# Cross-attention over a 1500-key context: maxima with keys as partitions, queries and output projection inside the batch loop, loops written out

## The reference

```python
h = (x - mean(x)) * rsqrt(var(x) + 1e-5) * gamma + beta
Q = split_heads(h @ Wq.T)                     # 32 heads of 16
K = V = split_heads(ctx)
scores = where(mask, einsum('bhsd,bhtd->bhst', Q, K) / 4, -inf)
attn = einsum('bhst,bhtd->bhsd', softmax(scores), V)
out = x + merge_heads(attn) @ Wout.T
```

## Time and profile before

| | |
|---|---|
| three runs | 1756.49 us median (1751.47 to 1764.45) |
| profiled execution | 1757.97 us, its span 1756.3 us |
| TensorE matmul busy | 1492.5 us, 85% |
| VectorE busy | 1064.4 us, 61% |
| GpSimd busy | 866.0 us, 49% |
| ScalarE busy | 722.4 us, 41% |
| mean granted TensorE clock | 0.936 of 2.4 GHz |
| HBM traffic | 126 GB/s over the span |

### The profile page before, as it was taken

How to read it: one execution, slowest core, us unless ns; L and a number is a source line. 1 busy time by engine, 2 the same in 40 slices (tenths; PEclk the granted TensorE clock), 3 DMA queues, 4 the chain that set the end, 5 groups by cost and what they waited for, 6 DMA issues and landing times.

```text
span 1756.3 us, 71565 instructions
## 1 busy us (share of the span) xinstructions
PE 1492.5 (85%) x31200; PEld 1097.7 (63%) x31200; DVE 1064.4 (61%) x3356; ACT 722.4 (41%) x495; POOL 866.0 (49%) x336
## 2 busy tenths in 40 slices
PE   4888989797988978798898879888797989889886
PEld 3336666565666666566666666666565666666665
DVE  5336767565765756576575657757565666656630
ACT  1114444444443434444343434434443444444443
POOL 1004555454555545555554545656454564555554
PEclk7889999999999989999998989999998999989899
DMA  9103434344443434444343444434334443434420
GB/s 282 33 1 140 141 131 143 113 156 132 141 146 119 138 104 155 133 141 148 119 142 101 154 132 143 151 122 152 118 121 140 147 155 117 149 109 136 138 79 12
DMA packets 41742, 225.45 MB, mean 128 GB/s; under 512 B 7106, under 2 KB 7138, under 8 KB 29442
## 3 DMA queue, kind: packets, MB, share of 16 engines
q1 hardware_dynamic: 41442, 220.79, 37.9%
HBM read 216.90 MB, written 3.77 MB: 126 GB/s over the span
## 4 chain that ended last, share of the span: by engine, by line
PE 57%; DVE 16%; ACT 11%; issue 8%; DMA 6%; SPq 2%; POOL 0%; ACTq 0%; POOLq 0%; DVEq 0%
PE ps L245 15%; DVE masked L299 12%; PE ps L225 12%; PE ps L260 11%; ACT probs L342 10%; PE ps L274 10%; DMA max_rows<-neg_maxT 5%; PE ps L653 4%; PE ps L236 3%; PE ps L285 3%; DVE den_inv L319 3%; SPq L193 2%; DMA v<-in_x 1%; ACT sums L612 1%; DVE tile_max L299 0%
## 5 line engine op out<-in xcount | busy, mean ns | idle before, releaser
L299 DVE CUSTOM_DVE_ANT_0 masked<-ps,mask_tile 112x500 bf16<-112x500 f32 x1536 | 969.0, 672 | 580.1 <-PE ps L225 578.8
L388 POOL TENSOR_TENSOR sums<-probs 125x1792 f32<-125x1792 f32 x192 | 767.3, 3997 | 865.3 <-ACT probs L342 865.3
L342 ACT ACTIVATE probs<-ps,mask_bias 125x1792 f32<-125x1792 f32 x384 | 673.9, 1755 | 886.8 <-PE ps L245 886.8
L225 PE MATMUL ps<-kT,qdb 32*112 32x500 bf16 x1536 | 517.7, 427 | 111.2 <-issue 63.7
L245 PE MATMUL ps<-qd,kT 32*125 32x112 f32 x12288 | 551.4, 284 | 29.7 <-issue 29.7
L245 PEld LDWEIGHTS ps<-qd,kT 32*125 32x125 f32 x12288 | 523.4, 192 | 32.1 <-issue 30.8
L260 PE MATMUL ps<-probs,v 125*32 125x112 f32 x12288 | 383.3, 267 | 1.1 <-ACT probs L342 1.1
L260 PEld LDWEIGHTS ps<-probs,v 125*32 125x32 f32 x12288 | 313.4, 113 | 73.4 <-issue 50.9
L225 PEld LDWEIGHTS ps<-kT,qdb 32*112 32x112 bf16 x1536 | 154.5, 126 | 251.5 <-DVE tile_max L299 126.5
L236 PE MATMUL ps<-max_rows,ones_row 1*125 1x448 bf16 x1536 | 180.6, 406 | 88.3 <-ACT probs L342 63.9
L274 PE MATMUL ps<-sums,ones 125*32 125x224 f32 x3072 | 202.6, 386 | 2.4 <-POOL sums L388 2.4
(11 more groups left out here) (39 smaller groups left out, 169.7 us busy)
## 6 DMA issues: line engine op xcount, KB each, us to landing
kT<-in_kt SPq DMA_DIRECT2D x96, 1000.0 KB, 6.0
v<-in_ctx SPq DMA_DIRECT2D x96, 1000.0 KB
mask_tile<-mask_add SPq DMA_DIRECT2D x32, 328.1 KB, 15.3
x_res<-in_x SPq DMA_DIRECT2D x16, 224.0 KB, 15.5
out<-result SPq DMA_DIRECT2D x16, 224.0 KB, 10.0
probs<-in_x SPq DMA_DIRECT2D x14, 224.0 KB, 9.0
max_rows<-neg_maxT SPq DMA_DIRECT2D x96, 1.0 KB
v<-in_wq_t SPq DMA_DIRECT2D x1, 1024.0 KB, 6.2
```

Source lines behind the costliest of these rows:

```text
L225: nc.tensor.matmul(ring[t % 2][0:PAIR_Q, 0:KEYS], qdb[rows, bt[1] % 2, g, :], keys, start=True, stop=True).then_inc(tile_scored, 1)
L299: nc.vector.tensor_tensor_reduce(out=masked[0:PAIR_Q, t % 2, :], in0=ring[t % 2][0:PAIR_Q, 0:KEYS], in1=mask_tile[0:PAIR_Q, bt[1] % 2, KEY ...
L342: nc.scalar.activation(probs[0:LANES, k % PROBS], ps[0:LANES, 0:TILES_R, 0:BANK_Q], ACT.Exp, bias=mask_bias[0:LANES, bass.ds(at, 1)], scal ...
L388: nc.gpsimd.tensor_tensor(sums[0:LANES, j % 2], probs[0:LANES, a], probs[0:LANES, a + 1], ALU.add).then_inc(summed, 1)
```

## The change

- **Maxima.** A tile is now one slot's 125 keys of one row group for all four blocks: four bf16 matmuls with the keys as weights and `qdb` as moving columns, output 125 keys x 448 queries. Two tiles (two row groups, both ring banks) are filled together, interleaved by block. VectorE adds the mask as a per-partition scalar and keeps a running maximum in `lane_max` (fp32, SBUF). At the end TensorE transposes `lane_max` (four transposes per row group), VectorE reduces over the 125 keys, TensorE transposes the 112 x 128 result once and VectorE spreads it over the blocks into `max_rows`. The mask tiles, their DMAs and the DMAs of the maxima are gone.
- **One ring.** Everything that VectorE takes from the two banks (maxima tiles, turned maxima, x, queries, output) is a unit of one list, `RING`; unit n waits until n-2 is taken, and TensorE and VectorE follow the list.
- **Queries and projection.** Before the first batch only the first pair's queries are made. The others are transposed and projected in slots 1 and 3 to 6 of an even batch, the output projection is cut into two units in slots 5 and 7 of an odd batch. Row statistics of the pairs 1 to 15 come from ScalarE.
- **Loops.** All loops are written out on every engine; no register stands in an address or a wait.

```diff
@@ units @@
+def slot_units(b, k):
+    n = TILES_R * (SLOTS - AHEAD_SLOT + k) if k < AHEAD_SLOT else TILES_R * (k - AHEAD_SLOT)
+    of = b + 1 if k < AHEAD_SLOT else b + 2
+    tiles = [("tile", of, n + j) for j in range(TILES_R)] if of < BATCH else []
+    behind_scores, behind_values = tiles[:2], tiles[2:]
+    if b + 1 < BATCH:
+        behind_values += [("turned", b + 1, r) for r in TURN_SLOTS.get(k, ())]
+        behind_values += [("rows", b + 1, 0)] if k == ROWS_SLOT else []
+    d = b // 2
+    if b % 2 == 0 and d + 1 < DOUBLES:
+        behind_values += [("x", d + 1, 0)] if k == X_SLOT else []
+        behind_values += [("q", d + 1, Q_SLOTS[k])] if k in Q_SLOTS else []
+    if b % 2 == 1 and d > 0:
+        behind_values += [("out", d - 1, OUT_SLOTS[k])] if k in OUT_SLOTS else []
+    return behind_scores, behind_values
@@ TensorE @@
-            nc.tensor.matmul(ring[t % 2][0:PAIR_Q, 0:KEYS], qdb[rows, bt[1] % 2, g, :], keys,
-                             start=True, stop=True).then_inc(tile_scored, 1)
+        def ring_bank(pe, unit):
+            n = RING_AT[unit]
+            wait_over(pe, ring_taken, n - 1)
+            return ps[:, 6 + n % 2, :]
...
+            return nc.tensor.matmul(bank[0:LANES, PAIR_Q * g:PAIR_Q * (g + 1)], keys, qdb[rows, b % 2, g, :],
+                                    start=(g == 0), stop=(g == BLOCKS - 1), skip_group_check=True)
+        def score_tiles(pe, units):
...
+                banks.append(ring_bank(pe, unit))
+            for g in range(BLOCKS):
+                for unit, bank in zip(units, banks):
+                    mm = score_tile(pe, unit, bank, g)
+                    if g == BLOCKS - 1:
+                        mm.then_inc(ring_filled, 1)
+        def turn_maxima(pe, unit):
+            _, b, r = unit
+            bank = ring_bank(pe, unit)
+            pe.wait_ge(ring_taken, taken(("tile", b, TILES - 1)))
+            for g in range(BLOCKS):
+                mm = nc.tensor.transpose(bank[0:PAIR_Q, LANES * g:LANES * (g + 1)],
+                                         lane_max[0:LANES, b % 2, r, PAIR_Q * g:PAIR_Q * (g + 1)],
+                                         ident[0:LANES, 0:LANES])
+            mm.then_inc(ring_filled, 1)
@@ TensorE's order @@
+            for b in range(BATCH):
+                for k in range(SLOTS):
+                    behind_scores, behind_values = slot_units(b, k)
+                    begin_scores(pe, b, k)
+                    score_slot(pe, b, k)
+                    fill_units(pe, behind_scores)
+                    if k >= 4 and k % 2 == 0:
+                        add_denominators(pe, b, k // 2 - 2)
+                    elif k in (0, 2) and b > 0:
+                        add_denominators(pe, b - 1, SUMS - 2 + k // 2)
+                    if k > 0:
+                        times_values(pe, b, k - 1)
+                    elif b > 0:
+                        times_values(pe, b - 1, SLOTS - 1)
+                    fill_units(pe, behind_values)
@@ VectorE @@
-            nc.vector.tensor_tensor_reduce(
-                out=masked[0:PAIR_Q, t % 2, :], in0=ring[t % 2][0:PAIR_Q, 0:KEYS],
-                in1=mask_tile[0:PAIR_Q, bt[1] % 2, KEYS * c:KEYS * (c + 1)], scale=1.0, scalar=LOWEST,
-                op0=ALU.add, op1=ALU.max, accum_out=tile_max[0:PAIR_Q, c, j:j + 1]).then_inc(tile_taken, 1)
+                nc.vector.scalar_tensor_tensor(most, bank[0:LANES, 0:BANK_Q], mask, most, ALU.add, ALU.max
+                                               ).then_inc(ring_taken, 1)
...
+            nc.vector.tensor_reduce(neg_max[0:PAIR_Q, r, 0:BLOCKS],
+                                    bank[0:PAIR_Q, 0:KEYS].rearrange("p (g m) -> p g m", g=BLOCKS),
+                                    AX_X, ALU.max, negate=True).then_inc(ring_taken, 1)
```

More of the change, by code:

```diff
@@ L210, in score_tile, with wait_over @@
[L210 to L221, removed]
+        def wait_over(eng, semaphore, count):
+            if count > 0:
+                eng.wait_ge(semaphore, count)
@@ new lines, in project_out, with fill_units @@
+        def project_out(pe, unit):
+            _, d, half = unit
+            bank = ring_bank(pe, unit)
+            pe.wait_ge(attn_ready, 2 * d + 2)
+            for g in range(BLOCKS):
+                mm = nc.tensor.matmul(bank[0:PAIR_Q, 0:HIDDEN // 2], attnT[:, g, :],
+                                      woutT[:, g, HIDDEN // 2 * half:HIDDEN // 2 * (half + 1)],
+                                      start=(g == 0), stop=(g == BLOCKS - 1))
+            mm.then_inc(ring_filled, 1)
+        def fill_units(pe, units):
+            tiles = [unit for unit in units if unit[0] == "tile"]
+            for n in range(0, len(tiles), 2):
+                score_tiles(pe, tiles[n:n + 2])
+            for unit in units:
+                if unit[0] == "turned":
+                    turn_maxima(pe, unit)
+                elif unit[0] == "rows":
+                    turn_rows(pe, unit)
+                elif unit[0] == "x":
+                    turn_x(pe, unit)
+                elif unit[0] == "q":
+                    project_q(pe, unit)
+                elif unit[0] == "out":
+                    project_out(pe, unit)
@@ L523, in _ @@
-            loop(pool, body)
-            add_heads(pool, end)
-            divide_heads(pool, end)
+            make_qdb(pool, 0)
+            make_qd(pool, 0)
+            make_qdb(pool, 1)
+            for b in range(BATCH):
+                for j in range(SUMS):
+                    sum_two(pool, b, j)
+                    if j == 0 and b + 1 < BATCH:
+                        make_qd(pool, b + 1)
+                    if j == 0 and b > 0:
+                        add_heads(pool, b - 1)
+                    if j == 1 and b > 0:
+                        divide_heads(pool, b - 1)
+                    if j == 2 and b + 2 < BATCH:
+                        make_qdb(pool, b + 2)
@@ L619, in _ @@
-            act.wait_ge(mask_added, 2)
-            def body(i, first, last):
-                for o in range(2):
-                    for k in range(SLOTS):
-                        exp_slot(act, (i, o), k)
-                        if k == 0 and not (first and o == 0):
-                            take_heads(act, (i, o - 1))
-            loop(act, body)
-            take_heads(act, end)
+            act.wait_ge(var_ready, 1)
+            nc.scalar.activation(rstd[0:PAIR_Q, 0:1], rstd[0:PAIR_Q, 0:1], ACT.Sqrt).then_inc(std_ready, 1)
```

769 lines of the change are left out of this document (334 added, 435 removed).

## The result

The changed kernel takes 2081.73 us (median of 4 runs, 2071.82 to 2089.61) against 1760.47 us of the kernel before on the same chips: 1.183 times as long, 95% interval 1.176 to 1.190. Slower was forecast, but 1870 us; the time lies far above the range.

The account below looks back on a forecast made before the run. Ring fills and takes in a row bound most slots, with units waiting behind them: 80 us start + 31 x 56.0 + 58 last batch - 6 = 1868, plus 1.7 outside, 1870 us; own range 1810 to 1930, 8-in-10 range 1695 to 1975.

Parts of the forecast that it names:

- fill and take in a row: Two-bank ring: a pair of tiles starts only when both banks are free, 1.75 us per pair, 3.50 per slot.
- the loop's stalls: TensorE's issue stalls at the loop's turn, with slow matmuls 8 to 10 us per pair of batches, vanish in straight code.
- The sum of a pair: Two batches of slots, units, reciprocals and normalising: 56.0 us a batch, 112.0 a pair against 101.7 before.
- the turning units: Turning the maxima in slots 9 and 10: waits behind tile pairs plus transposes, 4.6 us a batch.
- the four query units: Query projections through the ring: 0.83 us waiting plus 0.8 work each, 6.5 us per pair of batches.
- an output unit: One of two output projection pieces through the ring, 1.82 us of work, 2.65 us each per pair of batches.
- Granted clock near 1.00: Sign of being right: TensorE near full clock, without issue stalls over 2 us; 4.5 us added for 1.2 GHz at the start.
- GpSimd's sums keep 4.0 us in every 7 and stay hidden: GpSimd's sums were expected to delay nothing; no cost was put into the sum for them.
- Normalising at 0.2 us a batch: Normalising x on VectorE, 0.5 us once per pair of batches, counted as 0.2 us a batch.
- rival 3: Weight loads not hidden in their row group, fill 0.53 us, plus normalising waiting for GpSimd: 2010 us, chance 0.15.
- The take: VectorE's pass over 448 PSUM columns with an fp32 operand: 0.62 us, with 155 ns fixed.
- the fill: TensorE's four matmuls for each of two interleaved maxima tiles: 0.34 us per pair of tiles.

Follow-up runs that it names:

- a_attn2_actnorm: a_attn2 with x normalised by ScalarE instead of VectorE: 1975.7 us, 1.123 of the kernel before; run again 1977.78 us.
- a_attn2: The changed kernel with two buffers for attnT instead of one: 1993.3 us, 1.134 of the kernel before.
- a_single: a_attn2_actnorm with each maxima tile filled alone, waiting for its own bank only: 1770.5 us, 1.005 of the kernel before.
- a_filler6: a_attn2_actnorm with six unused matmul records ahead of x, query, output and each slot's first turning unit: 1925.42 us, 1.095 of the kernel before.
- a_half_take: a_attn2_actnorm with VectorE's running maximum over only 224 of 448 columns from a batch's second slot: 1749.79 us, 0.992 of the kernel before.
- b_unrolled: The kernel before with its loops written out on all engines, nothing else changed: 1685.56 us, 0.958 of the kernel before.

## Why the prediction was wrong

**The side and the reason for it were right.** The ring holds fill and take in a row: single tiles give back 205 us, half a take 226, and without the query units 137 go. The gain at the start came (first exp at 87 us, 80 forecast), the loop's stalls went.

**The sum of a pair was nearly right, but only for full clock and sums on time.** With the buffer and ScalarE's normalising (a_attn2_actnorm), and each of the 24 slots counted with its median at full clock over batches 2 to 29, exp to exp, a pair is 112.2 us; 112.0 was forecast. (Two slots beside the x unit have only one step at full clock each.) Against slots of 3.76 us, the turning units with the slot behind them cost 4.6 us a batch (4.6 forecast), the four query units 6.3 (6.5), an output unit 2.4 (2.65), and a slot without units is 0.08 over the forecast mean of 3.68. In the changed kernel a pair is 126.0 in the mean. Of the 14 us over the forecast, its own medians at full clock put 3.5 into the slot in which exp waits for the late sums and 2.1 into the slot with normalising; the mean lies 8.5 above the sum of the medians, and that is the clock. These are estimates, read from the steps of exp in one trace each. They say that the forecast failed in what it left out, and the clock is the largest part.

**"Granted clock near 1.00" failed.** I took the 1.2 GHz of the kernel before for a mark of its loop's stalls of 2 to 4 us, and gave it only to the start of the new one. Measured: 420 us at 1.2 GHz, in the estimate above some 130 of the 212 us between 1870 and 2082. Pauses of under 0.9 us bring it too: in a_attn2_actnorm no longer pause stands ahead of 42 of the 44 falls, counted as above. Filling part of the pauses gave 52 us there; the share in the changed kernel was not measured apart.

**"GpSimd's sums keep 4.0 us in every 7 and stay hidden" failed.** The output units were moved from slot 8 to slots 5 and 7, and I priced their records, but did not ask who waits for the last of them: `divide_heads`, which GpSimd reaches in slot 3, with sums behind it in the queue. Its wait is in the changed code in plain sight. Measured: 262.8 us of waiting on GpSimd, 185.7 on ScalarE, 88 us of time, by a_attn2, the clock's answer included.

**Normalising at 0.2 us a batch failed.** It is 2.77 us each where GpSimd sums. The forecast had the mechanism in rival 3 at up to 2.6 us a pair and 40 us, and left it out of the sum. Moved off VectorE it gave 18.

**The take was mis-sized, and another term made up for it.** 0.62 us from 155 ns of fixed part; it is 0.676, and a pair of tiles 1.87 instead of 1.75. The slots without units are longer by this, 1.9 us in a pair of batches; output, query and x units and the reciprocals came out cheaper by about as much, so that 112.2 against 112.0 is in part luck. With the fill I was right in size (0.34, the trace has 0.33 to 0.35 for eight weight loads) and rival 3 was wrong: with four loads in a row in one row group a_single has a record every 0.06 us, not 0.132. The Trainium skill (TensorE: Matmul & The Clock Gate, Part 3) lets weight loads pass running matmuls only where the row group differs. The trace of a_single does not bear this out for these records, and the interleaving by hand that it speaks for brought nothing here.

Sum: 88 + 18 + 52 of the 212 us have a run behind them. The rest, some 54, is by the estimate above nearly all in the 188 us at 1.2 GHz that a_filler6 still has: its pairs are 115.8 us in the mean and 112.9 with medians at full clock, 2.8 us a pair or 44 in 15.5 pairs. This is read from the trace and has no run by itself.

**The stalls of the loop** were put at 8 to 10 us a pair in the account of before. Straight code gains 5.3 a pair, and 9.5 once the DMAs of the maxima are moved. Part of what I had booked as loop was cover for another wait.

## What to carry to other kernels

When a step is moved, list who waits for its end, engine by engine, and what stands behind the waiter in its queue: a buffer with one copy that is refilled early in the order and read late holds up everything behind it. Take a slot's buffers one at a time, each with its own wait, unless a measured row shows that taking them together is faster; with two buffers, waiting for both makes one of them. Of a new order ask not only how long TensorE works but what pauses it gets: here pauses under 0.9 us also cost through the clock. And a written-out loop is cheap to try on the kernel that one has: here it gave 4%, and 7% with four small DMAs moved ahead in their queue.

## What the runs showed of the hardware

- A VectorE pass that reads 448 fp32 columns of PSUM, a per-partition scalar and an fp32 operand takes 676 ns, and 444 ns with 224 columns (a_half_take): 1.04 ns a column and some 210 ns fixed. Reading 500 columns and a bf16 operand had taken 672, which at the same rate leaves some 155 ns.
- An fp32 pass of VectorE from SBUF to SBUF, 546 ns alone, takes 2450 to 3010 ns beside one of GpSimd's 4.0 us sums and ends 0.3 us behind the sum; the same work on ScalarE takes 800 ns.
- Two maxima tiles in different row groups, four matmuls each, run side by side (0.46 us for eight) even when all four of one stand ahead of the other's in the program; four in one row group take 0.44 us.
- TensorE falls to 1.2 GHz behind pauses of 0.5 to 0.9 us, without a longer one (42 of 44 falls in a_attn2_actnorm); 52 us came back by giving it useless work in them (327 to 188 us at 1.2 GHz).
- A straight stream of 73 thousand TensorE instructions (the changed kernel) runs with no issue stall over 1.6 us between the first exp and the last. The kernel before has, as a loop, one of 3.99 and one of 2.18 us in a turn, and written out (b_unrolled) one of 2.60 between the first exp and the last.
